# A decoder layer in one program on one core: the entries of five stages rearranged, the identity kept on the chip, work cut into finer pieces at the borders

## The chip, the cores and the metric

The kernel runs on one core of one Trainium2 chip. TensorE (PE) multiplies matrices and also turns tiles by multiplying with an identity, VectorE (DVE), ScalarE (ACT) and GpSimd (POOL) work on elements, SyncE (SP) issues the transfers. The metric is the device time of one launch in microseconds (us); less is better.

## The reference

2048 tokens (4 sequences of 512) of width 512 pass one layer of three parts, each behind a norm and added to its input:

```python
x = x + _L0_attn_ref(_layernorm(x, axis=-1), ...)            # gated delta rule, 16 heads of 128
x = x + _L0_xattn_ref(_layernorm(x, axis=-1), ctx_2048, ...) # cross attention, quantised to 8 bits
x = x + _L0_ffn_ref(_layernorm(x, axis=-1), ...)             # self attention with rope, then 8 experts

# _L0_attn_ref: k, q, v are projections through a causal convolution of 4 taps and a silu
def step(Sstate, inputs):
    q_t, k_t, v_t, g_t, beta_t = inputs
    retrieved = jnp.einsum('bhkv,bhk->bhv', Sstate, k_t)
    error = v_t - g_t[..., None] * retrieved
    update = k_t[..., :, None] * (beta_t[..., None] * error)[..., None, :]
    Snew = g_t[..., None, None] * Sstate + update
    o_t = jnp.einsum('bhkv,bhk->bhv', Snew, q_t)
    return (Snew, o_t)
...
    o = o * jax.lax.rsqrt(jnp.mean(o * o, axis=-1, keepdims=True) + EPS) * norm_w
    o = o * jax.nn.silu(x @ Wg.T)
    return o @ Wo.T

# _L0_ffn_ref: q, k, v = h @ wq, h @ wk, h @ wv; rmsnorm; then
rot = rot * cos + rotate_half(rot) * sin      # the first 64 of each head's 128 columns
...
_, topi = jax.lax.top_k(sig + router_bias, TOPK)   # 2 of 8 experts for each token
```

## The kernel before

The program is a row of stages. Each stage is a block with one hand-written instruction stream for each engine; a block ends with a barrier of all engines, so nothing of a stage starts before all of the stage ahead has ended. What is needed across a border lies in memory of the chip or in DRAM. The streams are synchronised by counting semaphores only, and within an engine the order is that of the code.

- `front` normalises x and loads tables and the first head's raw weights.
- `delta_heads` works through 16 heads in 4 chunks of 128 positions, 64 steps ("slots") in all, as a software pipeline over three chunks. A head's four weight matrices (`JK`, `JQ`, `JG`, `JV`) are turned on PE against the identity (`turn_weights`) and split by ACT and DVE into a leading and a remaining part (`lead_weights`, `rest_weights`), so that three products of short-mantissa type give one of full precision (`project`, 12 matmuls). For a chunk, k is projected, copied (`copy_pre`), convolved by DVE in taps, passed through silu and turned (`gd_kT`); its product with itself gives a triangular matrix `gd_Lo`, which SP stores to DRAM and fetches back as blocks of 16x16; POOL inverts them in 15 steps (`start_solve`, `solve`), and the inverse goes through DRAM too before PE uses it. `row(cur_k, ...)` copies the head's convolution and decay numbers for the engines. The entry of the stage is code of its own: four weights, then the slots (-1, 1), (-1, 2), (-1, 3) that fill the pipeline.
- `delta_out` turns Wo in 16 pieces and multiplies it by the heads' outputs in 16 tiles. `leads` and `rests` split the loaded outputs into parts (`go_og_lead`, `go_og_rest`), 4 quarters a tile.
- `cross_tiles` is the cross attention in 16 tiles; its first step normalises a tile, turns it (`turn_x`) and multiplies by Wq (`queries`).
- `self_project` normalises, projects to q, k, v with weights again split in two parts (`lead_w` on ACT, `rest_w` on DVE, the first one on POOL), applies rope on POOL and turns the result (`turn_rotated`), in 16 tiles.
- `self_attention` is the causal attention; behind the attention of a batch, DVE routes the tokens of the batch before it in small steps between heads.
- `moe_sparse` runs 39 tiles of 128 token rows sorted by expert. A table of tiles (which expert, which row) is computed on DVE; the 17 tiles known to be full before the last batch is routed come first.

Each of `delta_heads`, `delta_out`, `cross_tiles` and `self_project` loads the 128x128 identity from DRAM for itself at its start; three of them wait for it before anything is turned, and two make a bf16 copy:

```python
for j, col in enumerate((C_ID, C_GT, C_LV + 64 * MERGE_AT)):      # delta_heads, SP
    sp.dma_start(cst[:, j * P:(j + 1) * P], const_dram[:, col:col + P]).then_inc(cst_in, 16)
...
dve.wait_ge(cst_in, 16)                                            # delta_out, DVE
nc.vector.tensor_copy(identb[:, :], ident[:, :]).then_inc(ident_ready, 1)
```

## Time and profile before

| | us |
|---|---|
| median of 3 runs (lowest, highest) | 3485.53 (3484.13, 3486.45) |
| the profiled execution | 3486.66 |
| its span | 3484.9 |
| PE busy in the span | 3238.8 (93%) |
| DVE, ACT, POOL busy | 2171.7, 1904.6, 1642.8 |

The span is the time between the first and the last record of the profiled execution. A granted TensorE clock of 1.00 is its full level, 2.4 GHz; 0.50 is the other, 1.2 GHz. By the times of their first instructions, `delta_heads` begins at 80.65, `delta_out` at 1765.40, `cross_tiles` at 1962.47, `self_project` at 2264.52, `self_attention` at 2596.33 and `moe_sparse` at 3207.15.

### The profile page before, as it was taken

Reading aid. Unit: us, or ns where it says so; the run is one execution under the profiler, and the core shown is the slowest. Engines: PE = TensorE matmul, PEld = TensorE weight load, DVE = VectorE, ACT = ScalarE, POOL = GpSimd, SP = SyncE. Lnnn points to the kernel's source line nnn. Section 1 sums busy time; section 2 is a strip of 40 time slices with the busy share of each in tenths; the row PEclk is TensorE's granted clock in tenths of the full one; section 3 lists DMA queues with packets and bytes.
Section 4 is the critical chain, followed back from the end, with each engine's and each line's share of the span. In section 5 each row is a group of like instructions: output and inputs, shape, how many; then the busy total and the mean of one; then the engine's idle time right before and its main releaser. Section 6 shows DMA issues by size and latency. Waiting matters only on the chain. (4 is left out here: it accounts for less than half of the span.)

```text
span 3484.9 us, 61218 instructions
## 1 busy us (share of the span) xinstructions
PE 3238.8 (93%) x19346; PEld 2593.4 (74%) x19346; DVE 2171.7 (62%) x4837; ACT 1904.6 (55%) x4656; POOL 1642.8 (47%) x3095
## 2 busy tenths in 40 slices
PE   6799999999999999999989788789979999998996
PEld 3688888888888888888878555478866777776543
DVE  5476776767767676776653488765437567584432
ACT  3577677776776777677632277644436455362111
POOL 2677877777787777777630000045543001111322
PEclk8799999999999999999999899999989999999998
DMA  4222222222222222222253323424342111212854
GB/s 116 57 62 59 67 71 67 62 73 64 59 67 68 70 62 71 67 59 67 83 170 96 126 112 139 171 95 121 96 150 93 67 67 68 104 62 78 242 98 90
DMA packets 432617, 314.87 MB, mean 90 GB/s; under 512 B 130256, under 2 KB 347600, under 8 KB 431216
## 3 DMA queue, kind: packets, MB, share of 16 engines
q1 hardware_dynamic: 424256, 293.96, 28.0%
q0 software_dynamic: 8176, 18.88, 2.7%
q8 instruction: 63, 1.03, 0.1%
q14 instruction: 122, 1.00, 0.1%
HBM read 182.36 MB, written 134.62 MB: 91 GB/s over the span
## 5 line engine op out<-in xcount | busy, mean ns | idle before, releaser
L634 PE MATMUL gd_PJ<-xn_lead,gd_w_rest 128*128 128x512 f32 x1024 | 421.6, 412 | 0.0
L634 PE MATMUL gd_PJ<-xn_lead,gd_w_lead 128*128 128x512 f32 x1024 | 403.5, 394 | 0.0
L634 PE MATMUL gd_PJ<-xn_rest,gd_w_lead 128*128 128x512 f32 x1024 | 402.0, 393 | 0.0
L1076 POOL TENSOR_TENSOR gd_T<-gd_T,gd_prod 32x14 f32<-32x14 f32 (+6 forms) x896 | 317.1, 354 | 70.2
L1073 POOL TENSOR_TENSOR gd_prod<-gd_L,gd_T 32x14 f32<-32x14 f32 (+6 forms) x896 | 295.8, 330 | 70.2
L799 DVE SCALAR_TENSOR_TENSOR gd_conv<-gd_pre,gd_cur_a,gd_conv 128x512 f32<-128x512 f32 x384 | 293.5, 764 | 9.6 <-ACT gd_conv L957 2.7
L634 PEld LDWEIGHTS gd_PJ<-xn_lead,gd_w_lead 128*128 128x128 f32 x1024 | 193.7, 189 | 43.7
L634 PEld LDWEIGHTS gd_PJ<-xn_lead,gd_w_rest 128*128 128x128 f32 x1024 | 194.4, 190 | 37.6
L634 PEld LDWEIGHTS gd_PJ<-xn_rest,gd_w_lead 128*128 128x128 f32 x1024 | 194.7, 190 | 35.3
L2516 ACT ACTIVATE sa_E<-sa_B,sa_nmax 128x512 f32<-128x512 f32 (+3 forms) x256 | 131.7, 526 | 133.4 <-DVE sa_nmax L2643 133.4
L932 DVE SCALAR_TENSOR_TENSOR gd_og<-gd_B,ptab,gd_gate 128x512 f32<-128x512 f32 x64 | 48.1, 751 | 247.3 <-PE gd_B L648 247.3
L643 PEld LDWEIGHTS gd_B<-gd_Y,gd_T 128*128 128x128 f32 (+1 forms) x1536 | 159.8, 174 | 29.0 <-issue 22.3
L799 DVE SCALAR_TENSOR_TENSOR gd_conv<-gd_pre,gd_cur_k,gd_conv 128x512 f32<-128x512 f32 x192 | 164.3, 856 | 21.8 <-ACT gd_conv L957 20.0
L643 PE MATMUL gd_B<-gd_W,gd_Lo 128*128 128x64 f32 (+1 forms) x1536 | 173.1, 256 | 4.5 <-DMA gd_T<-inverse_image 4.4
L643 PE MATMUL gd_B<-gd_Y,gd_T 128*128 128x64 f32 (+1 forms) x1536 | 174.4, 257 | 2.7 <-DVE gd_Y L814 1.0
L643 PEld LDWEIGHTS gd_B<-gd_W,gd_Lo 128*128 128x128 f32 (+1 forms) x1536 | 159.8, 174 | 16.0 <-issue 15.5
L956 ACT COPY gd_pre<-gd_PJ 128x512 f32<-128x512 f32 x192 | 112.2, 584 | 103.8 <-PE gd_PJ L634 80.1
L2486 PE MATMUL sa_B<-sa_wo_lead,sa_o_parts 128*128 128x512 f32 x512 | 162.2, 393 | 0.0
L1941 PE MATMUL sp_B<-sp_w_lead,sp_h_rest 128*128 128x512 f32 x384 | 157.4, 410 | 3.8 <-DVE sp_h_rest L2186 3.8
L2415 PE MATMUL sa_B<-sa_k_parts,sa_q_parts 128*128 128x512 f32 (+2 forms) x576 | 141.4, 367 | 19.4 <-DVE sa_q_parts L2674 12.0
L2437 PE MATMUL sa_B<-sa_PT,sa_v 128*128 128x512 f32 (+3 forms) x512 | 149.0, 434 | 6.8 <-DVE sa_PT L2651 6.8
L1941 PE MATMUL sp_B<-sp_w_lead,sp_h_lead 128*128 128x512 f32 x384 | 151.2, 394 | 0.0
(463 smaller groups left out, 8792.5 us busy)
## 6 DMA issues: line engine op xcount, KB each, us to landing
expert_rows<-xt_blank SPq DMA_DIRECT2D x16, 2112.0 KB, 7.3
turned_queries_keys<-f_wq SPq DMA_DIRECT2D x16, 1280.0 KB, 6.0
x_wo<-decay_sums SPq DMA_DIRECT2D x64, 256.0 KB, 3.7
triangles<-gd_Lo SPq DMA_DIRECT2D x64, 256.0 KB, 3.4
gd_W<-turned_image SPq DMA_DIRECT2D x64, 256.0 KB, 2.8
gd_T<-inverse_image SPq DMA_DIRECT2D x64, 256.0 KB, 3.3
gated_outputs<-gd_og SPq DMA_DIRECT2D x64, 256.0 KB, 2.8
go_ogt<-gated_outputs SPq DMA_DIRECT2D x16, 1024.0 KB, 5.9
```

The source lines that it names most:

```text
L634: mm = pe.matmul(bank, w_parts[wp][:, j, k, :], rhs, start=(k == 0 and wp == 1), stop=(k == KT - 1 and wp + xp == 0))
L643: mm = pe.matmul(bank[:, b, :], lhs[b], rhs[b], start=True, stop=True)
L799: nc.vector.scalar_tensor_tensor(out=conv[:, j], in0=pre[:, parm, j, :, d:d + P], scalar=cur[:, 4 * j + d:4 * j + d + 1], in1=conv[:, j], ...
L932: nc.vector.scalar_tensor_tensor(out=og[:, par, :], in0=Bk[0][:, :, :].rearrange("p b t -> p (b t)"), scalar=ptab[:, bass.ds(i, 1), PN:PN ...
L956: nc.scalar.copy(pre[:, parm, j, :, 3:3 + P], bank)
L1073: nc.gpsimd.tensor_tensor(prod[:, rows, 0:j], L16[:, rows, j:j + 1].to_broadcast(shape), T16[:, j:j + 1, 0:j].to_broadcast(shape), ALU.mul ...
L1076: nc.gpsimd.tensor_tensor(T16[:, rows, 0:j], T16[:, rows, 0:j], prod[:, rows, 0:j], ALU.subtract).then_inc(solving, 1)
L1941: mm = pe.matmul(bank[:, :], h_parts[hp][:, s, k, :], w_parts[wp][:, k, j, :], start=(k == 0 and hp == 1), stop=(k == KT - 1 and hp + wp = ...
L2415: pe.matmul(Bk[bank][:, col:col + w], q_parts[:, h % 2, qp, rows], k_parts[:, kp, h // REP, 0:w], start=(qp == 1), stop=False)
L2437: mm = pe.matmul(Bk[6 + h % 2][:, kk * P:SEQ], v[:, kk, kv * DH:(kv + 1) * DH], PT[:, h % 2, PT_AT[kk]:PT_AT[kk] + w], start=(kk == 0), st ...
L2486: mm = pe.matmul(Bk[Y_BANKS[i]][:, :], part(o_parts, h, op)[:, i * P:(i + 1) * P], wo_parts[wp][:, h, :], start=(h == 0 and op == 1), stop ...
L2516: ex = nc.scalar.activation(E[:, par, E_AT[i]:E_AT[i] + w], Bk[bank][:, col:col + w], ACT.Exp, bias=nmax[:, par, i:i + 1], accum_out=sums[ ...
```

## The change

1. The identity and its bf16 copy are allocated outside the stages (`ids`). `front` loads the one on SP behind the second load of x and makes the other on POOL. The loads, waits and casts of four stages go.
2. Entry of `delta_heads`: after turning `JK` and `JQ` PE projects k of chunk 0 before it turns `JG` and `JV`; ACT copies k's projection between the leads of `JQ` and `JG`; DVE makes the rest of `JV` behind the k taps of slot (-1, 2); POOL makes both row copies as its first work; SP issues the decay sums' row first, and the second one ahead of the next head's weights. The loop of the steady state is as before.
3. Entry of `delta_out`: each quarter of the first tile's outputs is split right after four pieces of Wo, where before all four quarters followed eight pieces.
4. Entry of `cross_tiles`: Wq comes in four loads with a semaphore each, and the first product waits piece by piece. POOL's first addition does not wait for the identity.
5. Entry of `self_project`: ACT loads the table of Sqrt by a 1-column activation first and puts the statistics of tile 0 and its `lead_h` between the leads of the weights; DVE norms tile 0 before the statistics of tile 1 and does all five `rest_w` after tile 0's rest; POOL's rest of weight 0 is cut in four, and PE waits for each.
6. Last tile of `self_project`: DVE does the rope of heads 0 to 11, POOL that of the other 8; PE starts to turn when DVE is done.
7. The table of the 17 early tiles is computed by DVE in the last batch of `self_attention` (steps h = 13 and h = 14) instead of at the start of `moe_sparse`; there SP fetches the first two tiles' rows ahead of the experts' weights.

```diff
@@ front, SP and POOL @@
             load_x(1)
+            sp.dma_start(ids[0][:, :], const_dram[:, C_ID:C_ID + P]).then_inc(ids_in, 16)
...
+            pool.wait_ge(ids_in, 16)
+            nc.gpsimd.tensor_copy(ids[1][:, :], ids[0][:, :])
@@ delta_heads, SP @@
-            for j, col in enumerate((C_ID, C_GT, C_LV + 64 * MERGE_AT)):
+            sp.dma_start(row_sums[:].rearrange("p b t -> p (b t)"), rows_dram[0, 0].rearrange("b t -> (b t)").partition_broadcast(P)).then_inc(row_in, 16)
+            for j, col in enumerate((C_GT, C_LV + 64 * MERGE_AT)):
...
-            sp.dma_start(row_sums[:].rearrange("p b t -> p (b t)"), rows_dram[0, 0].rearrange("b t -> (b t)").partition_broadcast(P)).then_inc(row_in, 16)
-            sp.wait_ge(image_in, 64)
+            load_row(-1, 1)
             sp.wait_ge(w_turned, 4)
             load_weights(1)
-            load_row(-1, 1)
+            sp.wait_ge(image_in, 64)
@@ delta_heads, PE @@
-            pe.wait_ge(cst_in, 48)
-            for j in range(4):
-                if j in (JV, JG):
-                    pe.wait_ge(w_copied, j)
-                turn_weights(0, j)
-            slots(pe, slot)
+            turn_weights(0, JK)
+            turn_weights(0, JQ)
+            pe.wait_ge(w_copied, 1)
+            project(JK, 0, k_proj)
+            pe.wait_ge(w_copied, 2)
+            turn_weights(0, JG)
+            pe.wait_ge(k_pre, 1)
+            turn_weights(0, JV)
+            slots(pe, slot, 2)
@@ delta_heads, ACT @@
-            for j in range(4):
-                lead_weights(0, j)
+            lead_weights(0, JK, 0)
+            lead_weights(0, JQ, 1)
+            act.wait_ge(head_k, 1)
+            act.wait_ge(k_proj, 1)
+            copy_pre(0, PK, JK, cur_k, k_pre)
+            lead_weights(0, JG, 2)
+            lead_weights(0, JV, 3)
@@ delta_heads, POOL @@
-                if has2 and c == 2:
+                if has2 and c == 2 and back:
                     row(cur_k, h2, head_k)
-                if has1 and c == CH - 1:
+                if has1 and c == CH - 1 and back:
                     row(cur_a, h1, head_a)
...
+            row(cur_k, 0, head_k)
+            row(cur_a, 0, head_a)
@@ delta_out, ACT (DVE likewise) @@
             for q in range(HQ):
-                if q == 2:
-                    leads(0, 0, 0)
                 for n in pieces(q):
...
+                if q == 0:
+                    act.wait_ge(tile_in[0], 16)
+                lead(0, 0, q)
@@ cross_tiles, SP and PE @@
-            sp.dma_start(wq[:, :, :], X["Wq"].rearrange("(k p) n -> p k n", p=P)).then_inc(wq_in, 16)
+            for k in range(KT):
+                sp.dma_start(wq[:, k, :], X["Wq"][k * P:(k + 1) * P, :]).then_inc(wq_in[k], 16)
...
-            queries(0, range(KT))
+            for k in range(KT):
+                pe.wait_ge(wq_in[k], 16)
+                queries(0, (k,))
@@ self_project, ACT @@
+            nc.scalar.activation(warm[:, :], eps[:, 0:1], ACT.Sqrt)
             lead_w(0)
+            roots_x(0)
             lead_w(1)
-            roots_x(0)
+            lead_h(0, 0)
             lead_w(2)
-            lead_w(3)
-            lead_h(0, 0)
-            lead_w(4)
             roots_x(1)
-            lead_w(5)
+            for j in range(3, NW):
+                lead_w(j)
@@ self_project, DVE: the entry, and the rope of the last tile @@
             moments(0)
+            norms(0, 0)
             spreads(1, 1)
-            norms(0, 0)
-            moments(1)
-            rest_w(1)
             scale_h(0)
...
-            for j in range(2, NW):
+            moments(1)
+            for j in range(1, NW):
                 rest_w(j)
...
+                if left == 0:
+                    hs = slice(0, SHARED)
+                    dve.wait_ge(q_weighed, t * QN + QN)
+                    for lo, hi in ((0, half), (half, ROT)):
+                        src = (lo + half) % ROT
+                        tt = nc.vector.tensor_tensor(sw[:, hs, lo:hi], qk[s][:, hs, src:src + half],
@@ self_attention, DVE, last batch @@
+                        elif h == 13 and not more:
+                            round_tiles(nc, then, R, -63.5)
+                            sum_tiles(nc, then, R)
+                        elif h == 14 and not more:
+                            tile_owners(nc, then, R, 0, EARLY)
+                            tile_rows(nc, then, R, 0, EARLY)
@@ moe_sparse, SP @@
-            load_weights(0)
+            sp.wait_ge(R.owned, 1)
             sp.wait_ge(R.sent, 16 * 2 * CH * last)
-            sp.wait_ge(owned, 1)
             load(0)
             load(1)
+            load_weights(0)
             load_weights(1)
```

Three places of the program show what the text moves. The first is PE at the entry of `delta_heads`, where `gd_PJ` holds turned weights (L625, against the identity) and projections (L634). Before:

```order
L625 MATMUL gd_PJ<-gd_cst,x_wo 128x128 x16
L634 MATMUL gd_PJ<-xn_lead,gd_w_rest 128x512
L634 MATMUL gd_PJ<-xn_rest,gd_w_lead 128x512
L634 MATMUL gd_PJ<-xn_lead,gd_w_lead 128x512
...
L643 MATMUL gd_B<-gd_kT 128x128 x4
```

And after:

```order
L627 MATMUL gd_PJ<-x_ident,x_wo 128x128 x8
L636 MATMUL gd_PJ<-xn_lead,gd_w_rest 128x512
L636 MATMUL gd_PJ<-xn_rest,gd_w_lead 128x512
L636 MATMUL gd_PJ<-xn_lead,gd_w_lead 128x512
...
L627 MATMUL gd_PJ<-x_ident,x_wo 128x128 x8
L645 MATMUL gd_B<-gd_kT 128x128 x4
```

Eight of the sixteen turnings now stand behind the twelve matmuls of the first projection.

The second is POOL in the same place; L1092 to L1097 are the arguments of a chunk's decay factors, made from the row of decay sums. Before, the row copy `gd_cur_k` stood behind two chunks' arguments, of which the second four rows are:

```order
L1092 TENSOR_TENSOR gd_tiny<-gd_none 128x4
L1094 TENSOR_TENSOR x_wo<-x_wo,ptab 128x512
L1096 TENSOR_TENSOR x_wo<-x_wo,gd_cst 128x512
L1097 TENSOR_TENSOR x_wo<-x_wo,gd_never 128x512
L1048 COPY gd_cur_k<-ptab 128x116
```

After, both row copies stand ahead of all else that POOL does in the stage:

```order
L1060 UNCONDITIONAL_BRANCH
L1063 COPY gd_cur_k<-ptab 128x116
L1063 COPY gd_cur_a<-ptab 128x116
L1152 MEMSET gd_o 128x4
L1153 MEMSET x_osq 128x16
```

The copy no longer waits behind anything that waits for a transfer.

The third is SP at the start of `moe_sparse` (`ms_xr` are a tile's rows, `ms_wgu` and `ms_wd` an expert's weights). Before:

```order
L2827 DMA ms_wgu<-in_L_ffn_wg 128x4x256
L2827 DMA ms_wgu<-in_L_ffn_wu 128x4x256
L2828 DMA ms_wd<-in_L_ffn_wd 128x2x512
L2840 TENSOR_LOAD ms_row_i
L2840 ISA x2
L2841 ISA
L2841 DMA ms_xr<-expert_rows 128x528
```

And after:

```order
L2930 TENSOR_LOAD ro_first_i
L2930 ISA x2
L2931 ISA
L2931 DMA ms_xr<-expert_rows 128x528
...
L2917 DMA ms_wgu<-in_L_ffn_wg 128x4x256
L2917 DMA ms_wgu<-in_L_ffn_wu 128x4x256
L2918 DMA ms_wd<-in_L_ffn_wd 128x2x512
```

Two fetches of rows now come before the first expert's three loads.

## Rows read from the trace of the kernel before

**Rows 1.** The page: busy time, share of the span and instructions of the engines.

```profile
PE 3238.8 (93%) x19346; PEld 2593.4 (74%) x19346; DVE 2171.7 (62%) x4837; ACT 1904.6 (55%) x4656; POOL 1642.8 (47%) x3095
```

**Rows 2.** Busy time by stretch; the columns are named in the first row.

```profile
core 0: us, PE busy (x) PEld busy (x) DVE busy (x) ACT busy (x) POOL busy (x), PEclk, DMA share, GB/s
160.00:1745.00 1585.00, 1575.38 (x10931) 1391.46 (x10930) 1114.56 (x2429) 1106.96 (x2603) 1189.26 (x2676) 1.00 0.26 67
2300.00:2575.00 275.00, 275.00 (x1383) 229.27 (x1381) 136.10 (x230) 112.71 (x285) 152.39 (x72) 1.00 0.35 106
```

**Rows 3.** Timeline, entry of `delta_heads`: start, us, engine, line, operation, [idle before it, releaser].

```profile
80.65 1.28 SPq L583 DMA_DIRECT2D gd_cst<-in_const  x3
...
83.68 1.12 PE L625 MATMUL gd_PJ<-gd_cst,x_wo 128*128 128x128 f32 x4 [7.32 <-DMA gd_cst<-in_const]
...
89.55 0.20 POOL L1092 TENSOR_TENSOR gd_tiny<-gd_none 128x4 f32<-128x4 f32 x1 [6.55 <-DMA x_wo<-decay_sums]
...
90.33 0.78 PE L634 MATMUL gd_PJ<-xn_lead,gd_w_rest 128*128 128x512 f32 x1
...
101.27 0.59 ACT L956 COPY gd_pre<-gd_PJ 128x512 f32<-128x512 f32 x1 [6.74 <-POOL gd_cur_k L1048]
...
102.66 4.04 DVE L799 SCALAR_TENSOR_TENSOR gd_conv<-gd_pre,gd_cur_k,gd_conv 128x512 f32<-128x512 f32 x3 [10.63 <-ACT gd_conv L957]
...
107.42 2.08 PE L643 MATMUL gd_B<-gd_kT 128*128 128x128 f32 x8 [12.24 <-ACT gd_kT L961]
```

**Rows 4.** Timeline, first blocks solved in `delta_heads`.

```profile
117.45 0.82 POOL L1063 TENSOR_TENSOR gd_T<-gd_L,gd_below 32x256 f32<-32x256 f32 x1 [9.63 <-DMA gd_L<-triangles]
118.23 0.73 POOL L1048 COPY gd_cur_a<-ptab 128x116 f32<-128x116 f32 x1
...
139.36 1.94 PE L643 MATMUL gd_B<-gd_W,gd_Lo 128*128 128x64 f32 x8 [4.40 <-DMA gd_T<-inverse_image]
```

**Rows 5.** Timeline, PE at the entry of `delta_out`.

```profile
1767.31 1.97 PE L1282 MATMUL go_psK<-go_ident,x_kf 128*128 128x128 f32 x8 [7.03 <-DMA go_ident<-in_const]
...
1777.49 0.76 PE L1274 MATMUL go_psY<-go_wo_lead,go_og_rest 128*128 128x512 f32 x1 [2.09 <-DVE go_og_rest L1339]
```

**Rows 6.** DMA issues of that entry: KB each, median us to landing.

```profile
go_ogt<-gated_outputs SPq DMA_DIRECT2D x2, 1024.0 KB, 8.2
...
go_ident<-in_const SPq DMA_DIRECT2D x1, 64.0 KB, 1.9
```

**Rows 7.** Timeline, PE at the entry of `cross_tiles`.

```profile
1966.04 1.08 PE L1521 MATMUL xt_T<-xt_ident,xt_xn 128*128 128x128 f32 x4 [7.73 <-DVE xt_xn L1703]
...
1968.58 5.20 PE L1528 MATMUL xt_Q<-xt_wq,xt_xT 128*128 128x512 f32 x8 [1.46 <-DMA xt_wq<-in_L_xattn_Wq]
```

**Rows 8.** DMA issues, a load of 256 KB in 88:97.

```profile
x_wo<-in_L_attn_Wk SPq DMA_DIRECT2D x1, 256.0 KB, 2.6
```

**Rows 9.** Timeline, entry of `self_project`.

```profile
2272.83 2.28 DVE L2180 TENSOR_TENSOR sp_w_rest<-f_wq,sp_w_lead 128x2048 fp32r<-128x2048 f32 x1
...
2277.14 0.79 PE L1941 MATMUL sp_B<-sp_w_lead,sp_h_rest 128*128 128x512 f32 x1 [3.79 <-DVE sp_h_rest L2186]
...
2290.55 0.60 PE L1935 MATMUL sp_B<-sp_ident,sp_hn 128*128 128x128 f32 x4
```

**Rows 10.** Line L2121, DVE: duration ns min/median/max, first and last start.

```profile
L2121 DVE TENSOR_SCALAR sp_hn<-sp_xn,sp_st x16: 486/3052/3067, 2271.6 to 2546.4; 128x512 f32<-128x512 f32 x16
```

**Rows 11.** Timeline, last rope of `self_project`.

```profile
2580.63 3.06 POOL L2090 TENSOR_TENSOR f_wk<-f_wq,sp_rope 128x640 f32<-128x640 f32 x2 [9.50 <-DVE f_wq L2162]
...
2589.74 4.21 PE L1958 MATMUL sp_B<-sp_ident,f_wq 128*128 128x128 f32 x20 [7.20 <-POOL f_wq L2097]
```

**Rows 12.** Timeline, entry of `moe_sparse`.

```profile
3212.66 1.89 SPq L2841 DMA_DIRECT2D ms_xr<-expert_rows  x2
...
3215.29 1.11 PE L2940 MATMUL ms_T<-ro_ident,ms_xr 128*128 128x128 f32 x4 [11.71 <-DMA ms_xr<-expert_rows]
...
3221.13 1.45 PE L2995 MATMUL ms_G<-ms_wgu,ms_hT 128*128 x3
```

**Rows 13.** DMA issues of that entry.

```profile
ms_wgu<-in_L_ffn_wu SPq DMA_DIRECT2D x2, 512.0 KB, 5.3
```

More of the change, by code:

```diff
@@ L770, in slot @@
                     pe.wait_ge(v_pre, n + 4)
-                    if c == 2 or not back:
+                    if not back:
+                        pe.wait_ge(w_copied, 4)
+                    elif c == 2:
                         pe.wait_ge(w_copied, (i + 1) * 4 + JV + 1)
@@ L844, in slot @@
                     tap(n + 2, par, PK, cur_k, (2,), k_tap)
+                if not back and c == 2:
+                    rest_weights(0, JV, 3)
                 if back and c > 0:
@@ L1971, in slot @@
                         pe.wait_ge(q_weighed, (t - 1) * QN + j + 1)
-                    project(Bk[j], s, j, range(KT), q_sum)
+                    project(Bk[j], s, j, range(KT), q_sum, head and j == 0)
                 if second(t):
@@ new lines, in tile_owners @@
+def tile_owners(nc, then, R, lo, n):
+    at, now = slice(lo, lo + n), R.after[:, lo:lo + n, :]
+    then(nc.vector.tensor_tensor(now, R.used[:, 1].unsqueeze(1).to_broadcast([P, n, EXPERTS]), bc(R.order[:, 0:n], EXPERTS), ALU.is_le))
+    then(nc.vector.tensor_reduce(R.owner[:, at], now, AX.X, ALU.add))
+    then(nc.vector.tensor_scalar(R.owner[:, at], R.owner[:, at], float(EXPERTS - 1), None, ALU.min))
+    then(nc.vector.tensor_copy(R.owner_i[:, at], R.owner[:, at]))
+    then(nc.vector.tensor_scalar(R.owner_key[:, at], R.owner[:, at], -1.0, float(EXPERTS), ALU.mult, ALU.add))
+    then(nc.vector.tensor_scalar(R.gap[:, :], R.whole[:, :], -float(P), float(TOK), ALU.mult, ALU.add))
@@ L3115, in _ @@
                     pick_expert(nc, then, R, last, 1)
-                    nc.vector.tensor_tensor(R.two[:], R.pick[:, 0, R.tiles(last), :], R.pick[:, 1, R.tiles(last), :], ALU.add).then_inc(chosen, 1)
+                    nc.vector.tensor_tensor(R.two[:], R.pick[:, 0], R.pick[:, 1], ALU.add).then_inc(chosen, 1)
                 elif j == 2:
```

314 lines of the change are left out of this document (155 added, 159 removed).

## The prediction, made before the result was known

> **What bounds the kernel now.** I read the page first. PE is busy 93% of the span, far ahead of DVE [rows 1]. Then busy time by stretch, to see where PE's other 246 us lie. The long loops hold little of it: in the heads' loop PE works 1575.38 of 1585.00 us, in the middle of the self projection 275.00 of 275.00, both at the full clock [rows 2]. So a microsecond saved at such a stage's entry isn't given back inside it: what follows is a queue of PE work that starts earlier and runs at the same pace. The waits to win are single ones, at the borders, where the barrier leaves every engine empty. The timeline of each border shows them. In the delta stage's entry ACT waits 6.74 us for POOL's row copy and PE then 12.24 us for the turned k [rows 3]; after that PE waits for the first inverse [rows 4]. At the next border PE waits 7.03 us for the identity, part of which is the barrier [rows 5]; in the cross stage 7.73 for the first normed tile [rows 7]; in the self projection for `sp_h_rest` [rows 9]; at its end 7.20 for POOL's rope [rows 11]; in the expert stage 11.71 for the first rows [rows 12]. The change works at these six places, so I sum six terms. A term is the shift of the first instruction behind which PE no longer waits.
>
> **Delta entry: 11.0 us (9.5 to 11.8).** Before, PE can start only when three constants have landed, at 83.68 [rows 3]. After, it needs what `front` left and the semaphore that SP raises behind three issues. The three took 1.28 us in all, and the row's issue is a longer one; I take PE's start as 82.45. The first turning, its split and the wait for `w_copied` took from 83.68 to PE's second batch about 2.5 us; so the projection of k starts near 84.95 instead of 90.33 [rows 3]. Its twelve matmuls cost 4.8 us then (0.78 for the first, at half clock); I let them cost the same and end at 89.7. ACT could copy at once, since `gd_cur_k` is made at the stage's start. Before, it stood behind the arguments of two chunks, on POOL, the first of which waited for the decay sums until 89.55, and the copy on ACT came at 101.27 [rows 3]. From that copy to the first product with the turned k it took 107.42 − 101.27 = 6.15 us, with three taps of 4.04 in it. After: 89.7 + 6.15 = 95.9 if nothing is in the way. But now the taps fall beside POOL's arguments, and ACT has two leads and the tables of its functions to pass between; I add 1.3 and take 97.2, a shift of 10.2. From there the chain is fixed: triangle, store, fetch, POOL's solve from 117.45, two trips through DRAM, PE at 139.36 [rows 4]. It shifts whole, and POOL's `gd_cur_a` copy of 0.73 us, which stood between its first blocks and the solve, is gone: 0.8 more. PE's own work in between fits: it was idle for half of the stretch. The low bound has the taps slowed and ACT's turns in the way (1.5 less), the high one neither (0.8 more). The moved transfers: the next head's weights are requested some 3 us later, behind the fourth turning, and wanted only a whole head later; the second row comes earlier, which only helps.
>
> **Delta_out entry: 3.0 us (2.0 to 3.6).** The identity took 1.9 us to land [rows 6]; PE starts that much sooner than 1767.31 [rows 5]. The first product stood behind eight pieces of Wo and the outputs' split on ACT and DVE and began at 1777.49. After, only four pieces precede it, but the outputs must be there: two loads of 1024 KB land after a median of 8.2 us [rows 6], the first earlier than the second, and they're issued 0.4 us sooner. Landed near 1772.7, a lead and a rest of 0.6 each and their waits: product at 1774.5. If the two loads share the engines evenly the gain is 2.0; if the first lands alone, 3.6. The remaining pieces keep pace with PE.
>
> **Cross entry: 3.0 us (2.0 to 3.3).** Two waits lie in a row. The first tile was normed behind the identity's load and its cast on DVE, 1.9 + 0.2 us; without them the turning moves from 1966.04 to about 1963.9. Then the products waited for all of Wq until 1968.58 [rows 7]. In four loads the first 256 KB come sooner: such a load landed after 2.6 us elsewhere [rows 8], issued now at 1962.5, and the others follow an issue of 0.4 each, the last near 1966.5. So the products start near 1965.6, when the turned tile is copied. They run at half clock in 5.20 us, so each piece of k (1.3 us) is there before it is wanted. The low bound has the pieces late, one issue each.
>
> **Self projection's entry: 2.0 us (1.1 to 2.7).** The first product comes at 2277.14, behind `rest_w(1)` of 2.28 us that DVE does ahead of PE's turned tile, and a table load and a second lead on ACT [rows 9]. Both leave that path, and product 0 moves up to 3.3 us. But PE isn't free then: DVE now has five rests of 2.28, 11.4 us, behind tile 0's, and only then norms tile 1, whose turning stood at 2290.55 [rows 9]. By DVE's queue (2275.0 + moments + 11.4 + norm) it comes at 2288.5. So 2.0 and not 3.3.
>
> **Last rope: 4.0 us (3.3 to 6.3).** POOL works from 2580.63 until PE starts at 2589.74 [rows 11], 9.1 us for 20 heads. For 8 heads that is 3.6, with its waits about 4.0. DVE's 12 heads, by 2.28 us for 2048 columns [rows 9], cost 2 x 0.43 + 2 x 0.86, with waits 3.1. In parallel PE starts at 2583.7, 6 us sooner. But both read the memory together. What that costs can be bounded: the same 512-column instruction took DVE 486 ns at the least and 3052 ns in the median [rows 10], and the latter is the length of one full-width rope instruction (POOL's 9.1 us hold two of these and two of half the width). So I expect the two to alternate, DVE's last instruction ending near 2586.1: gain 3.6. Some overlap is likely, since not every wait falls on the other's work: 4.0. PE then turns 12 heads (2.5 us) while POOL ends, so the second part costs nothing. The Trainium skill ("SBUF — State Buffer", "Who interferes with whom") has the same as a rule: GpSimd and VectorE share one pair of ports, under an exclusive lock. By that rule the term would be 3.6, and the rule speaks against item 6 and against cutting POOL's rest of weight 0.
>
> **Expert entry: 3.7 us (2.5 to 4.5).** The rows of tiles 0 and 1 were requested at 3212.66, when DVE had the table [rows 12]. With the table made before, they're requested at 3208.3 (the barrier at 3207.15, two register loads), and PE turns them 4.4 us sooner, at 3210.9. The first expert product, 3221.13 [rows 12], waits besides for weights whose loads are now behind the rows: issued near 3210, the slower half landing after some 6 or 7 us (5.3 in the median [rows 13]), so 3217.4. That gives 3.7. The 21 added instructions of some 0.2 us each on DVE in the attention fall into gaps of about 2 us between heads, where DVE waits; if that cover were gone they'd cost 4.2.
>
> **Nothing:** the identity's extra load in `front` is one issue of 0.4 us ahead of weights whose product isn't ready to start for another microsecond; the Sqrt table and the issues on SP lie under waits for transfers.
>
> **The sum.** 11.0 + 3.0 + 3.0 + 2.0 + 4.0 + 3.7 = 26.7. The profiled execution took 3486.66, so 3460.0; the median of the runs shown is 1.1 below it: 3459. Taking all low bounds gives 20.4, all high ones 32.2.
>
> **The rivals.** (a) *Another wait takes the delta entry's place, 12%.* The projection must wait for something I don't see, or POOL's arguments and ACT's tables push k's taps to 101 instead of 97: 6 us are gained there, or less, and the others as said: 3464 to 3472. For it: three engines' queues are all reordered and the chain has a single DVE, ACT and POOL. Against: PE's idle time before 107.42 was longer than 11. (b) *More, 13%.* Rope on two engines really in parallel (+2), the clock's lower level left sooner since PE waits less, first product of the self projection carrying its 3.3: 3446 to 3452. Against: rows 10. (c) *No change, 3%.* The steady loops aren't bound by PE's queue but by something that a late start hid, a DVE or POOL that then is waited for; the shift is given back. Then the time is 3479 to 3486. Against: 1575 of 1585 us. (d) *Slower, 2%.* The slots of the heads' loop settle into another pattern, since the loop now starts with DVE and POOL in another relation to PE. 61 slots, 26.7 + 7 us to lose: each must wait 0.55 us more than now to pass 3493. PE's waits in the loop are 9.6 us in 61 slots, 0.16 each, so such a pattern would be seen as a new wait several times as large: 3495.
>
> **How the numbers follow.** My sum holds with 70%, by its bounds 3453 to 3465. The range must leave out at most 2 in 10: it takes in half of (a) and most of (b) on either side: 3451 to 3468. A measurement of this kernel tells about 0.2% (7 us) from no change; below 3478.5 lie the sum, (a) and (b): 95%, within 3%, slower 2%.
>
> **What would show it.** Right: PE's first projection at 85, ACT's copy of k at 90, PE's product with the inverse at 128 to 129, the loop's waits as now; cross products at 1965.6 less the shift; the last turning's wait of 3.5 us and DVE instructions of the rope as long as POOL's; expert product 0 about 10.3 us after its barrier. Wrong: an ACT copy of k that waits for anything but the projection, `sp_hn` of tile 1 not moved, a new wait for weights in the expert stage above 4 us, or a loop longer than 1585 us for the same slots.

## The result and the profile after

The changed kernel takes 3467.45 us, median of 6 runs (3466.14 to 3473.19), against 3485.99 of the kernel before (6 runs, 3484.13 to 3488.66). That is 18.5 us less by the two medians. The ratio is 0.995, with a 95% interval of 0.9939 to 0.9961, so 13.6 to 21.3 us less and not 26.7. The median lies 8.5 us above the 3459 that I named, at the slow edge of my range of 3451 to 3468. In two later comparisons, each with its own runs of the kernel before on the same chip, the same kernel stood at 0.9932 (0.9920 to 0.9945) and 0.9937 (0.9922 to 0.9953), so 22 to 24 us less. The kernel is faster by 0.5 to 0.7%, and by less than I said. The profiled execution took 3466.85 us with a span of 3465.0.

All stages are parted by barriers, so the profile can be cut there. The table holds the time from each stage's first record on a computing engine to the next stage's, in us. "Before" gives the kernel before in two profiles, and the change is taken from their mean; "first after" is the first profile of the changed kernel; the last column takes every profile in which that stage's code was as changed (the changed kernel three times, and the experiments that touch other stages).

| stage | before (two profiles) | first after | after, all profiles | mean change | my terms |
|---|---|---|---|---|---|
| front | 80.8, 80.3 | 80.3 | 79.5 to 81.8 | +0.3 | 0 |
| delta | 1684.7, 1683.0 | 1673.2 | 1672.0 to 1675.0 | -10.6 | -11.0 |
| delta_out | 197.0, 196.7 | 192.6 | 192.4 to 192.6 | -4.4 | -3.0 |
| cross | 302.1, 301.9 | 305.2 | 298.3 to 305.5 | +0.4 | -3.0 |
| self projection | 331.7, 331.8 | 325.1 | 325.1 to 326.9 | -5.6 | -6.0 |
| self attention | 610.9, 609.8 | 610.5 | 608.7 to 611.0 | +0.1 | 0 |
| experts | 277.7, 279.0 | 278.1 | 276.6 to 278.6 | -0.5 | -3.7 |

Two rows carry the miss, cross and experts. The timeline of the delta stage's entry after the change, which answers to [rows 3] and [rows 4]:

```profile
80.17 0.28 POOL L1063 COPY gd_cur_k<-ptab 128x116 f32<-128x116 f32 x1 [16.02 <-POOLq L55]
...
81.53 1.97 PE L627 MATMUL gd_PJ<-x_ident,x_wo 128*128 128x128 f32 x8 [5.65 <-SPq L588]
...
84.05 0.79 PE L636 MATMUL gd_PJ<-xn_lead,gd_w_rest 128*128 128x512 f32 x1 [0.55 <-DVE gd_w_rest L799]
...
89.67 0.59 ACT L966 COPY gd_pre<-gd_PJ 128x512 f32<-128x512 f32 x1 [5.55 <-PE gd_PJ L636]
...
92.06 2.84 DVE L806 SCALAR_TENSOR_TENSOR gd_conv<-gd_pre,gd_cur_k,gd_conv 128x512 f32<-128x512 f32 x3
...
96.73 2.08 PE L645 MATMUL gd_B<-gd_kT 128*128 128x128 f32 x8 [5.08 <-ACT gd_kT L971]
...
130.08 1.94 PE L645 MATMUL gd_B<-gd_W,gd_Lo 128*128 128x64 f32 x8 [4.03 <-DMA gd_T<-inverse_image]
```

ACT's copy now waits for the projection and no longer for POOL, and PE's first product with the turned k comes at 96.73 instead of 107.42. The taps stayed near their old place relative to it, and took 2.84 us instead of 4.04. The first product with the inverse is 9.3 us sooner, and the stage is 10 to 12 us shorter.

PE at the entry of delta_out, against [rows 5]:

```profile
1753.48 1.94 PE L1296 MATMUL go_psK<-x_ident,x_kf 128*128 128x128 f32 x8 [5.20 <-PEq L55]
...
1762.56 0.47 PE L1289 MATMUL go_psY<-go_wo_lead,go_og_rest 128*128 128x512 f32 x1
```

The stage starts at 1753.43, so the first product comes after 9.1 us instead of 12.1. The stage is 4.4 us shorter, and the other 1.4 us lie in the twelve products that follow. In the kernel before PE had waited 2.09 us ahead of them [rows 5], and they took 4.2 us at a mean granted clock of 0.65. In the changed kernel that wait is gone and they take 2.8 us at 1.00. Busy time by stretch, first before and then after (columns as in [rows 2]; the third last is the granted clock):

```profile
1777.50:1781.70 4.20, 4.20 (x12) 3.33 (x13) 1.65 (x3) 0.59 (x2) 0.00 (x0) 0.65 1.06 389
1762.60:1765.40 2.80, 2.80 (x14) 2.25 (x13) 1.97 (x4) 1.10 (x2) 0.00 (x0) 1.00 1.05 385
```

PE in the cross stage: the first turning and the first two products (answering to [rows 7]), and the last one.

```profile
1948.46 1.11 PE L1537 MATMUL xt_T<-x_ident,xt_xn 128*128 128x128 f32 x4 [6.47 <-DVE xt_xn L1718]
...
1950.34 6.43 PE L1544 MATMUL xt_Q<-xt_wq,xt_xT 128*128 128x512 f32 x8 [0.77 <-ACT xt_xT L1665]
...
1960.89 6.26 PE L1544 MATMUL xt_Q<-xt_wq,xt_xT 128*128 128x512 f32 x8
...
2241.29 6.02 PE L1588 MATMUL xt_Q<-x_wp,xt_oT 128*128 128x512 f32 x8 [0.77 <-ACT xt_oT L1685]
```

The product starts 4.2 us after the stage's start (1946.13), where it was 6.1; that part of the change works. But it lasts 6.43 us instead of 5.20, the second 6.26 and the last, which the change doesn't touch, 6.02. In the kernel before the latter two were:

```profile
1977.74 5.35 PE L1528 MATMUL xt_Q<-xt_wq,xt_xT 128*128 128x512 f32 x8
...
2256.94 3.67 PE L1572 MATMUL xt_Q<-x_wp,xt_oT 128*128 128x512 f32 x8 [0.77 <-ACT xt_oT L1670]
```

The same eight instructions take 3.67 us or 6 and more. Busy time by stretch shows why; the third last column is PE's granted clock, here of the changed kernel around its first products and at its last:

```profile
1946.10:1950.30 4.20, 1.11 (x4) 0.71 (x4) 2.38 (x6) 0.58 (x1) 3.31 (x4) 0.50 0.69 235
1950.30:1956.80 6.50, 6.46 (x10) 2.86 (x11) 0.11 (x1) 0.00 (x0) 0.00 (x0) 0.57 1.01 410
...
1960.90:1967.20 6.30, 6.25 (x10) 2.32 (x8) 0.01 (x1) 1.87 (x2) 0.00 (x0) 0.58 0.98 355
2241.30:2247.30 6.00, 6.00 (x8) 2.34 (x8) 0.00 (x0) 0.00 (x0) 0.00 (x0) 0.61 0.52 198
```

And of the kernel before:

```profile
1968.60:1973.80 5.20, 5.20 (x10) 2.39 (x11) 0.00 (x0) 0.00 (x0) 0.00 (x0) 0.71 1.01 424
...
2256.90:2260.60 3.70, 3.66 (x8) 1.44 (x8) 0.00 (x0) 0.00 (x0) 0.00 (x0) 1.00 0.98 376
```

So the clock stood at its lower level, 0.50 (1.2 GHz), for most of both first products, after PE had been idle for 6.5 us across the border, and rose to 1.00 within them. In the kernel before it rose earlier in the product's course. Two longer stretches, before and after, show where:

```profile
1962.50:1971.50 9.00, 4.01 (x8) 2.09 (x9) 2.35 (x7) 0.59 (x1) 3.35 (x4) 0.50 0.84 315
...
1946.10:1955.80 9.70, 6.57 (x11) 3.11 (x12) 2.48 (x6) 0.58 (x1) 3.31 (x4) 0.50 0.87 334
```

The clock was still at 0.50 for the first 9.0 us of the stage before the change and for the first 9.7 us after it. The product now starts 1.9 us sooner in the stage, but the clock doesn't return sooner. So more of the product falls under the lower level, and it ends only 0.7 us sooner, 10.6 us after the stage's start instead of 11.3.

The self projection, entry and last rope, against [rows 9] and [rows 11]:

```profile
2261.97 6.68 DVE L2213 TENSOR_TENSOR sp_w_rest<-f_wq,sp_w_lead 128x2048 fp32r<-128x2048 f32 x3
...
2275.02 0.66 PE L1950 MATMUL sp_B<-x_ident,sp_hn 128*128 128x128 f32 x4
...
2566.41 1.37 DVE L2194 TENSOR_TENSOR f_wq<-f_wq,sp_rope 128x768 f32<-128x768 f32 x1
...
2567.04 1.85 POOL L2113 TENSOR_TENSOR f_wq<-f_wq,sp_rope 128x512 f32<-128x512 f32 x1
2567.81 1.90 DVE L2197 TENSOR_TENSOR f_wq<-f_wq,f_wk 128x768 f32<-128x768 f32 x1
...
2568.97 1.86 POOL L2116 TENSOR_TENSOR f_wq<-f_wq,f_wk 128x512 f32<-128x512 f32 x1
2569.86 4.13 PE L1976 MATMUL sp_B<-x_ident,f_wq 128*128 128x128 f32 x20 [2.91 <-DVE f_wq L2197]
```

Tile 1's turning comes 23.8 us after the stage's start instead of 26.0. This profile is a lucky one at that place: the same turning came at 23.8 once more (the experiment with three pieces put back), and at 25.0 in the eight other profiles with the new entry. The difference is DVE's norm of tile 0, which runs beside POOL's pieces of weight 0. Here it is in the first profile, and in the second one of the changed kernel:

```profile
2255.93 0.55 DVE L2139 TENSOR_SCALAR sp_xn<-sp_xt,sp_mv,sp_st 128x512 f32<-128x512 f32 x1
...
2251.79 1.65 DVE L2139 TENSOR_SCALAR sp_xn<-sp_xt,sp_mv,sp_st 128x512 f32<-128x512 f32 x1
```

In the two profiles with 0.55 us, POOL's second piece took 1.51 and 1.55 us; in the eight with 1.52 to 1.65 us it took 1.27. One of the two engines was held up each time. PE's wait ahead of the last turnings is 2.91 us instead of 7.20 in every profile of the changed kernel.

The expert stage, against [rows 12], and a wait that the kernel before didn't have:

```profile
3190.65 1.11 PE L3027 MATMUL ms_T<-ro_ident,ms_xr 128*128 128x128 f32 x4 [7.79 <-DMA ms_xr<-expert_rows]
...
3197.56 4.07 PE L3082 MATMUL ms_G<-ms_wgu,ms_hT 128*128 x8 [0.34 <-SPq L2922]
...
3242.70 1.12 PE L3027 MATMUL ms_T<-ro_ident,ms_xr 128*128 128x128 f32 x4 [2.56 <-DMA ms_xr<-expert_rows]
```

From the stage's start at 3186.89 the first product comes after 10.7 us instead of 14.0, as foretold. But 56 us into the stage PE waits 2.56 us for the rows of tile 8, and the stage as a whole takes 0.4 us more than in the first profile of the kernel before, and 0.9 less than in the second.

### The profile page after: what moved, and what is told of

Its sections match the earlier page's. It is cut to its first block and busy times, and to the rows that moved or that the text cites. A ratio compares the mean times of both kernels' runs of the same rounds, so it can differ in the third digit from the quotient of the medians.

```text
span 3465.0 us, 61217 instructions
## 1 busy us (share of the span) xinstructions
PE 3242.1 (94%) x19346; PEld 2594.6 (75%) x19346; DVE 2173.4 (63%) x4839; ACT 1901.3 (55%) x4657; POOL 1640.4 (47%) x3099
## 5 line engine op out<-in xcount | busy, mean ns | idle before, releaser
L1088 POOL TENSOR_TENSOR gd_prod<-gd_L,gd_T 32x14 f32<-32x14 f32 (+6 forms) x896 | 280.3, 313 | 71.0
L806 DVE SCALAR_TENSOR_TENSOR gd_conv<-gd_pre,gd_cur_a,gd_conv 128x512 f32<-128x512 f32 x384 | 300.7, 783 | 9.6 <-ACT gd_conv L967 2.7
L2511 PE MATMUL sa_B<-sa_k_parts,sa_q_parts 128*128 128x512 f32 (+2 forms) x576 | 142.6, 370 | 18.5 <-DVE sa_q_parts L2773 11.9
```

The lines of the kernel that those rows point to most:

```text
L806: nc.vector.scalar_tensor_tensor(out=conv[:, j], in0=pre[:, parm, j, :, d:d + P], scalar=cur[:, 4 * j + d:4 * j + d + 1], in1=conv[:, j], ...
L1088: nc.gpsimd.tensor_tensor(prod[:, rows, 0:j], L16[:, rows, j:j + 1].to_broadcast(shape), T16[:, j:j + 1, 0:j].to_broadcast(shape), ALU.mul ...
L2511: pe.matmul(Bk[bank][:, col:col + w], q_parts[:, h % 2, qp, rows], k_parts[:, kp, h // REP, 0:w], start=(qp == 1), stop=False)
```

## The experiments

Two questions: is the cross stage's loss the clock or the change's own code, and why does the expert stage keep nothing of 3.3 us? Ten runs follow, seven of them of new kernels. Experiments start from the changed kernel unless they say otherwise; "stage" is measured as in the table above.

**The changed kernel again.** 

> The changed kernel once more, for the spread of its stages from one execution to the next. The stages in its first profile, against those of the kernel before: delta 11.5 us less, delta_out 4.4 less, cross 3.1 more, self projection 6.6 less, experts 0.4 more. Theory clock: the cross stage's loss is the clock, which stands at its lower level for both first products and for the last one; where a drop falls changes from execution to execution, so the stage comes out between 297 and 305 us. Rival: the cross stage's loss is in what the change does there (pieces of Wq, fewer waits) and comes out at 305 again, to 0.3.

3464.14 us, 0.9932 of the kernel before. The cross stage took 301.4 us with products of 6.24, 3.65 and 6.00; the other stages repeated to 1.7 us. Of the 3.8 us between this cross stage and the first profile's, 2.6 are the second product's clock.

**A third time, beside the last two experiments.** 

> The changed kernel a third time, beside the next two on the same chip. By both theories: cross stage 298 to 305 us, expert stage 277 to 279, 20 to 25 us less than the kernel before.

3466.78 us, 0.9937; cross 305.5 with 6.55, 6.32 and 5.97; experts 276.6. Both stages lie just outside what I had expected, on opposite sides.

**The kernel before again.** 

> The kernel before, for a second look at its stages. The first showed the cross stage at 302.1 us, with its two first products at 5.2 and 5.35 us and the last at 3.67, and the expert stage at 277.7. Theory clock: the cross stage comes out at another length of 300 to 307 us, differing by whole products at the one or the other level of the clock, while delta (1684.7) and delta_out (197.0) repeat to 1 us. Rival (the changed kernel's cross stage is longer by its code): 302.1 again, to 0.3.

3484.28 us in one run. The cross stage was 301.9 us with 5.13, 5.35 and 3.67: the rival's number, not mine, which asked for another length. The kernel before repeats this pattern in both of its profiles; the changed kernel varies. Five more profiles have its cross code unchanged or nearly so: 302.4 (6.39, 6.25, 3.67), 298.5 (6.19, 3.65, 3.67), 305.2 (6.45, 6.27, 6.02), 298.3 (6.03, 3.65, 3.67), and 304.7 with Wq in one load (below; 5.62, 5.35, 6.32). Taking the three products away, the changed stage is 285.0 to 286.7 us and the one before 287.8 (302.1 less 14.2), so 1.1 to 2.8 less: the entry's gain is there, and most of what varies on top are three products, each at the one or the other level of the clock. (The 1.7 us that the remainder varies go with them: it is 285.0 to 285.5 where the second product took 3.65 us, and 286.1 to 286.7 where it took 6.3.)

**Turnings that do nothing, through the cross stage's entry and its last gaps.**

```diff
+            def hum(out, n):
+                for _n in range(n):
+                    pe.transpose(out, ident[:, :], ident[:, :])
+
+            hum(psQ[:, 0:P], 8)
             turn_x(0)
+            hum(psQ[:, 0:P], 2)
...
+            hum(psS[0][:, 0, 0:P], 7)
             values(TILES - 1, 3)
+            hum(psS[0][:, 0, 0:P], 5)
             turn_o(TILES - 1)
+            hum(psS[0][:, 0, 0:P], 5)
```

with 20 more at the end of delta_out's PE stream. 

> The changed kernel with throw-away turnings of the identity on PE: 20 at the end of delta_out's stream, 8 ahead of the first turning in the cross stage, 2 behind it, 17 in the stage's last gaps. They write memory that nobody reads any more. Theory clock: with PE kept busy through the border the granted clock stays at 1.00, the first product takes 3.7 us instead of 6.4, the second 3.7 instead of 6.3, the last one 3.7 instead of 6.0, and the stage gets 6 to 8 us shorter, 297 to 299. Rival (the products wait for something else, transfers or ACT): the stage stays at 305, or longer by the added work of up to 1.5 us.

3459.61 us, 0.9920 (0.9907 to 0.9932), on the chip and against the same runs as the 0.9932 above. PE's timeline:

```profile
1942.21 2.34 PE L1319 MATMUL go_psW<-x_ident 128*128 128x128 f32 x20
1946.56 1.07 PE L1646 MATMUL xt_Q<-x_ident 128*128 128x128 f32 x8 [2.00 <-PEq L55]
1948.83 0.66 PE L1539 MATMUL xt_T<-x_ident,xt_xn 128*128 128x128 f32 x4 [1.21 <-DVE xt_xn L1729]
...
1950.26 3.67 PE L1546 MATMUL xt_Q<-xt_wq,xt_xT 128*128 128x512 f32 x8 [0.55 <-ACT xt_xT L1676]
...
1957.89 3.65 PE L1546 MATMUL xt_Q<-xt_wq,xt_xT 128*128 128x512 f32 x8
...
2234.33 3.67 PE L1590 MATMUL xt_Q<-x_wp,xt_oT 128*128 128x512 f32 x8 [0.22 <-ACT xt_oT L1696]
```

The busy time by stretch has the clock at 1.00 through both products:

```profile
1946.50:1950.30 3.80, 1.99 (x15) 1.57 (x15) 2.46 (x6) 0.59 (x1) 3.32 (x4) 1.00 0.73 233
1950.30:1953.90 3.60, 3.60 (x10) 1.63 (x11) 0.02 (x1) 0.00 (x0) 0.00 (x0) 1.00 0.89 296
```

All three products run in 3.67 us and the stage takes 295.5 us, 3 to 10 less than without. The first product starts 3.8 us after the stage instead of 4.2, behind the same waits. This decides for the clock and against the rival: neither transfers nor ACT hold the products.

**The first expert's weights ahead of the rows.**

```diff
+            load_weights(0)
             sp.wait_ge(R.owned, 1)
             sp.wait_ge(R.sent, 16 * 2 * CH * last)
             load(0)
             load(1)
-            load_weights(0)
             load_weights(1)
```

> The changed kernel with the first expert's weights requested ahead of the first two tiles' rows again, as before the change; the table is still made in the stage before. Theory transfers: in the first 50 us the expert stage is bound by the stream of the experts' weights, at a DMA share of 1.05 to 1.10, and what PE gains at the entry it waits for later at the rows of tile 9, which are requested behind the last weights. With the weights first the stream starts 2.4 us sooner after the stage's start, the wait of 2.6 us for the rows of tile 9 shrinks to 1 or less, and the stage takes 275 to 277 us instead of 278.1. Rival (order of the first rows matters more): PE starts 2 to 3 us later, and the stage is 278 to 280.

3465.36 us, 0.9937; expert stage 277.3 us. PE started 3.7 us later, since the rows landed behind the weights:

```profile
PE ms_T L3027 <- DMA ms_xr<-expert_rows: 11.5, 1, 11.5
```

(PE's waits in the stage: total, times, longest). Its first product came 12.7 us after the stage's start instead of 10.4 to 10.8, tile 7's at 57.3 (56.6 to 59.9 in the changed kernel's three profiles), and the stage was no longer than theirs. It lies between what the theory (275 to 277) and the rival (278 to 280) had said. A product that starts 2 us later didn't lengthen the stage. But the weights were also requested 2.6 us sooner here, so the run doesn't show by itself that the entry is without effect.

**Rows of tiles 9 to 11 ahead of the wait for the last weights.** The loop of `load(j)` from 9 to 11 was moved ahead of `landed(EXPERTS - 1)` on SP. 

> The changed kernel with the rows of tiles 9 to 11 requested ahead of the wait for the last expert's weights. Theory transfers: the wait of 2.6 us for the rows of tile 9 goes, and the drop of the clock behind it; the stage takes 274 to 276 us instead of 278.1. Rival (the three row loads only push the weights, or another wait takes its place): 277.5 to 279.

3467.56 us, 0.9940 (one of the six runs took 6156.73 us, at a granted clock of 0.866 in the mean; it has no profile and stays unexplained; the other five lie between 3458 and 3470, with a median of 3466.36); expert stage 276.3 us. I had named the wrong tile: the long wait stands before tile 8's rows, which are requested ahead of these, and it stayed at 1.15 us. Only a later wait of 1.1 to 1.3 us, seen in three other profiles for tile 9's rows, is gone. Inconclusive on the cause.

**The residual's loads behind the weights.** The four `xb` loads (1 MB) went behind the loop over the experts, and POOL's additions of them behind its scatter. 

> The changed kernel with the four loads of the last batch's residual (1 MB) requested behind all experts' weights, and POOL's additions of them behind its scatter. Theory transfers: the stream that PE waits for at tiles 7 and 8 gets 1 of some 16 MB shorter, at about 365 GB/s 2.8 us; PE's wait before tile 8's rows (1.1 to 3.4 us in five profiles) shrinks to under 1, tile 7's product comes at 54 to 56 us after the stage's start instead of 57 to 60, and the stage takes 274 to 276 us. Rival (PE's own queue is the bound and the wait at tile 8 an accident): 277 to 278.

3472.81 us, 0.9948; expert stage 284.2 us, 6 longer. Both theories missed it. The wait at tile 8 was still 2.02 us, and a new one of 5.78 us arose at tile 9: SP stores the base rows before it requests the rows of tile 9 and later, and the store now waited for POOL. What it does show: the last expert's weights were requested 1.4 to 2.2 us sooner, tile 6's product came at 47.8 instead of 49.3 to 49.7, and tile 7's at 57.6, no sooner than in the changed kernel (56.6 to 59.9). That points to something other than the length of that stream.

**The scatter behind the additions of tiles 2 to 5.** In the first profile the last of the last expert's three loads, requested 41.2 us after the stage's start, took 13.3 us to land. In the kernel before it was requested at 41.1 and took 9.4. POOL's eight indirect writes of the last batch's rows run beside it, and the change has brought them forward. The first of them, after and before:

```profile
3230.36 1.00 POOL L2986 DMA_INDIRECT expert_rows<-ro_h,ro_row_i  x1 [0.30 <-issue]
...
3252.98 1.01 POOL L2899 DMA_INDIRECT expert_rows<-ro_h,ro_row_i  x1 [0.30 <-issue]
```

This is 43.5 us after the stage's start instead of 45.8. PE had got ahead, so POOL's additions of tiles 0 and 1 came sooner, and the scatter behind them too. The requests for the last weights and for tile 8's rows had not moved.

```diff
-            add(0)
-            add(1)
+            for j in range(6):
+                add(j)
             pool.wait_ge(routed, 1)
...
-            for j in range(2, MT):
+            for j in range(6, MT):
```

> The changed kernel with POOL's scatter of the last batch's rows (eight indirect transfers, 2.1 MB) behind the additions of tiles 2 to 5 instead of ahead of them. Theory transfers: tile 7's product waits for the last expert's weights and tile 8's rows, which share the DMA engines with the scatter; without it they land 3 to 5 us sooner, PE's wait before tile 8's rows goes, tile 7's product comes 54 to 55.5 us after the stage's start instead of 57 to 60, and the stage takes 272.5 to 275.5 us instead of 277.4 to 278.6. Rival (the weights' own stream of 12.6 MB is the bound): 277 to 278.5. Rival (the late tiles' rows are late instead): a new wait near tile 17, 278 or more.

3462.79 us, 0.9933 beside 0.9937; expert stage 274.2 us. PE's waits in the stage:

```profile
PE ms_T L3027 <- DMA ms_xr<-expert_rows: 8.6, 2, 7.8
PE ms_A L3043 <- DVE ms_aT L3127: 2.9, 2, 2.5
```

Only the two waits of the entry are left of the first line; tile 7's product comes 55.5 us after the start, and the stage is 2.4 to 4.4 us shorter than with the scatter in its old place. The load of tile 8's rows shows why. It is requested 45 to 46 us after the stage's start in both kernels. In the changed kernel's first profile, and in this one (KB, us to landing):

```profile
ms_xr<-expert_rows SPq DMA_DIRECT2D x1, 264.0 KB, 9.8
...
ms_xr<-expert_rows SPq DMA_DIRECT2D x1, 264.0 KB, 6.0
```

In the changed kernel's third profile it took 9.0 us, and in the run of all pieces together (below), which also has the late scatter, 6.0. In the kernel before it took 6.7. Two limits remain. The medians don't separate this kernel from the changed one beside it: 3462.79 (3456 to 3467) and 3466.78 (3462 to 3469). And the stage is now 3.5 to 4.8 us shorter than in the kernel before, more than the entry's 3.3. A part of that is likely a loss that the kernel before had too: there tile 7's product followed tile 6's by 6.5 and 7.0 us, where the following tiles come every 5.8. The late scatter in the kernel before was not run.

**Three pieces put back, each in its own stage.**

```diff
-                if has2 and c == 2 and back:
+                if has2 and c == 2:
                     row(cur_k, h2, head_k)
...
-            row(cur_k, 0, head_k)
-            row(cur_a, 0, head_a)
@@ cross_tiles @@
...
-            for k in range(KT):
-                pe.wait_ge(wq_in[k], 16)
-                queries(0, (k,))
+            pe.wait_ge(wq_in[0], 16)
+            queries(0, range(KT))
@@ self_project @@
-        SHARED = 3 * REP
+        SHARED = 0
...
```

(and Wq in one load, `cur_a` likewise, without DVE's part of the rope). 

> The changed kernel with three pieces put back, each in a stage of its own: POOL's row copies stand behind the chunks' arguments again, Wq comes in one load with one wait, and the last rope is done by POOL alone. My prediction's sum: delta 3 to 5 us longer than 1673 (with the decay sums requested earlier, the row copy comes near 93 instead of 101); the cross stage's first product starts 6.1 us after the stage instead of 4.2, so 1.9 longer at the same clock; self projection 4.3 longer. Rival for delta: the row copies carry the whole of its gain, 10 us or more. Rival for the rope: the split gives less than 2 us, because DVE and POOL stand in each other's way.

3477.42 us, 0.9964. Delta takes 1678.4 us, 5.1 more than the changed kernel's mean (3 to 5 expected):

```profile
94.02 0.28 POOL L1063 COPY gd_cur_k<-ptab 128x116 f32<-128x116 f32 x1
94.33 0.59 ACT L966 COPY gd_pre<-gd_PJ 128x512 f32<-128x512 f32 x1 [9.27 <-POOL gd_cur_k L1063]
```

The row copy comes at 94.0 and ACT waits for it, as reckoned. So about half of the stage's gain is in POOL's two copies. That the rest lies in the order on PE and SP and in the identity is by subtraction; none of these was put back alone. The cross product started 5.7 us after the stage, 1.5 later (1.9 expected). The rope by POOL alone:

```profile
2576.84 2.88 POOL L2110 TENSOR_TENSOR f_wq<-f_wq,f_wk 128x1280 f32<-128x1280 f32 x1
2579.86 4.21 PE L1970 MATMUL sp_B<-x_ident,f_wq 128*128 128x128 f32 x20 [7.20 <-POOL f_wq L2110]
```

PE waits 7.20 us again instead of 2.91, so the split is worth 4.3 us. The stage was 329.5 us, 4.4 more than in the changed kernel's first profile, which has the same entry (tile 1's turning at 23.8) and last turnings of nearly the same length (4.13 and 4.21 us). Against the others it is 2.6 to 3.9 more, since their entry is slower and their last turnings take 3.29 or 4.67 us.

**All that helped, together,** with throw-away turnings also at the end of `front` (24), in the delta stage's entry (60) and ahead of the last rotated heads (14). 

> The changed kernel with the throw-away turnings of the cross stage's experiment, the late scatter, the rows of tiles 9 to 11 requested early, and further throw-away turnings: 24 at the end of the first stage, 60 in the delta stage's entry, 14 ahead of the last 20 turnings of the rotated heads. Theory clock: the first projection of k takes 2.8 us instead of 5.2, the first products with the turned k 1.1 instead of 2.1, so the delta stage is 2 to 5 us shorter than 1673; the last turnings 2.7 instead of 4.1 to 4.7; cross stage 295.5; in all 14 to 20 us less than the changed kernel. Rival: the delta chain waits for DVE, ACT and DMA alone and gains less than 1.5 us, and the whole is 10 us less.

3457.03 us, 0.9915 (0.9901 to 0.9928), the lowest median of all, 9.8 us below the changed kernel's median on that chip. Delta 1670.6 us: its first products with the turned k ran at the full clock, the second ones didn't, after PE had been idle for 6.89 us again (the granted clock was 0.50 from 108 to 112 us):

```profile
95.57 1.16 PE L647 MATMUL gd_B<-gd_kT 128*128 128x128 f32 x8 [1.25 <-ACT gd_kT L981]
109.09 2.08 PE L647 MATMUL gd_B<-gd_kT 128*128 128x128 f32 x8 [6.89 <-ACT gd_kT L981]
```

The cross stage was 297.8 us, with 5.73, 3.65 and 3.67: the same turnings that had held the clock before let it fall here, 1.5 us after the stage's start. The expert stage was 275.6 us, without a wait at tile 8, but 1.4 longer than with the scatter alone and only 1.0 shorter than the 276.6 beside it. Gains from both the turnings and the scatter are there, but not the 14 to 20 us that I named: the whole is the rival's 10.

## Why the prediction was wrong

**Delta entry, right.** The term was 11.0, and the stage is 10.6 us shorter in the mean. PE's first projection came at 84.05 (84.95 foretold), ACT's copy at 89.67 (89.7), the first product with k at 96.73 (97.2), and the inverse at 130.08, later than my 128.4. By the mean of eight profiles the product with the inverse came 9.7 us sooner, not 11.0. The stage's other 0.9 us lie behind it, and the two profiles of the kernel before differ there by 2.0. So about a microsecond of the agreement is luck. The heads' loop kept its pace, which puts out rivals (a), (c) and (d); no run came to the times of (b).

**Delta_out entry, the number right and the path not.** The first product is 3.0 us sooner, which is the term. I had written that "only four pieces precede it", but PE turned eight pieces ahead of it as before (the order on PE was not changed). PE starts 1.9 us sooner and no longer waits 2.09 us for the outputs' rest. The other 1.4 us of the stage's 4.4 are the clock in the first twelve products, which the sum put at nothing.

**Self projection, right in the sum.** First tile and rope together were 6.0, and 5.6 were measured. The entry gave 2.2 us in the first profile, but 1.1 in the seven others that count here, where I had said 2.0: DVE's norm beside POOL's cut rest took up to 1.65 us instead of 0.55. The rope gave 4.3, where I had said 4.0. That the two errors cancel is luck. DVE and POOL did alternate: DVE's two 768-column instructions took 1.37 and 1.90 us where I had reckoned 0.86 without POOL. The second of them began at 2567.81, while POOL's ran until 2568.89, and ended at 2569.71, 0.82 us after it. The Trainium skill ("SBUF — State Buffer", "Who interferes with whom") calls it an exclusive lock on a shared pair of ports; the trace agrees.

**Cross entry, the step that failed.** "They run at half clock in 5.20 us": I moved the product's start and took its length along. It became 6.0 to 6.5 us, the second one 3.65 or 6.3 where it had been 5.35, and the last of the stage 3.67 or 6.0. The mean of seven stages came out 0.4 us above before, 3.4 short of the term. Of these, 1.1 are the start. It moved by 1.9 us and not by 3.0, because the first turning, still waiting for the normed tile, moved by 1.2 and not by 2.1. The other 2.3 are the three products, 16.5 us together in the mean instead of 14.2. The experiment with throw-away turnings shows that their length is the clock: 295.5 us with the clock held up.

**Expert entry, the other step that failed.** The term ended at "the first expert product", 3.7 sooner; it measured 3.3, and the stage gave it all back but 0.5 us. I had written that behind an entry there's only "a queue of PE work that starts earlier", and showed it for two loops [rows 2], neither of which was this one. Some of it was lost early: tile 3's product came 1.9 us sooner than in the first profile before, not 3.3. The rest went 56 us into the stage, where PE waits for rows that are requested behind the last weights. They took 9.0 and 9.8 us to land with POOL's scatter beside them, and 6.0 twice with the scatter later. I had even named "a new wait for weights in the expert stage above 4 us" as a sign of error and given it no term; it came as a wait for rows, of up to 2.6 us in the changed kernel. Moving the scatter alone brought the stage to 274.2 in the one profile there is.

Both together are 3.4 and 3.2 us short. With 1.4 more in delta_out and small differences elsewhere, the mean of the profiles comes to 20 us less, against 26.7. My bounds for these two terms began at 2.0 and 2.5, so none of them let a gain vanish behind the entry; only rival (a) had such a loss, in the delta stage, the one place where there was none.

**Left open:** why the kernel before repeats its cross pattern while the changed one shows four, and when exactly the clock falls. The border's idle time is alike in both (6 to 8 us), and the same turnings held it once and once not. Also open is why the product with the inverse came later than the chain before it, and how much the late scatter would have given the kernel before.

## What to carry to other kernels

Follow a saved wait to the end of its stage before counting it. Ask which transfers run at a DMA share near 1 in the first tens of microseconds (1.07 to 1.08 from 10 to 50 us in the expert stage here), what PE will reach earlier than they allow, and what other engine's transfers the earlier start will bring forward onto them. A stage's first products after an idle border ran at the lower clock here, and starting one 1.9 us earlier made it 0.8 to 1.4 us longer. Cheap turnings of the identity in the gap may keep the clock up; they did in one of two kernels. Where stages are parted by barriers, two profiles of the same kernel tell which stage's length is stable enough to be argued with.

## What the runs showed of the hardware

The same eight matmuls of 512 columns took 3.65 to 3.67 us at a granted clock of 1.00 and up to 6.55 when it stood at 0.50 for most of them, and which of these a product got changed between executions of the same kernel. That spreads the cross stage over 7 us in the profiles. The changed kernel's runs lie between 3460.9 and 3473.2 us, and those of the kernel before between 3484.1 and 3491.1; that the clock is the reason for the wider spread is likely but not shown, since only one execution of each set has a profile. A 264 KB load took 9.0 and 9.8 us to land beside POOL's indirect writes and 6.0 without them. Cutting POOL's rest of weight 0 into four made it 5.29 to 5.41 us instead of 4.51, with DVE's instructions beside it.
